# Layer 1 of a four-layer decoder on one Trainium2 core: half 0 of the cross attention centred and projected amid half 1's recurrence

## What is computed

```
# L1_attn, a gated linear recurrence
gate, u = split(x @ Wi)
u = causal_conv4(u) + conv_b
forget, inp = split(u @ Wg + bg)
alpha = exp(-8 * softplus(forget_base) * sigmoid(forget))
beta = sqrt(1 - alpha**2 + 1e-6)
h[t] = alpha[t] * h[t-1] + beta[t] * sigmoid(inp[t]) * u[t]
x = x + (gelu(gate) * h) @ Wo

# L1_xattn, on the normalized x, 16 heads (a reshape without a transpose)
Q, K, V = xn @ Wq + bq, ctx @ Wk + bk, ctx @ Wv + bv
x = x + softmax(causal(Q K^T * sqrt(8))) V
```

## Time and profile before

| | us |
|---|---|
| median of 3 runs (lowest to highest) | 1304.92 (1300.38 to 1306.22) |
| the profiled execution: time | 1302.31 |
| the profiled execution: span of the trace | 1300.4 |
| layer 1, half 1's gates to the first scores | about 444 to 480 in the trace |
| layer 1, attention steps | about 479 to 567 in the trace |

### The profile page before, as it was taken

How to read it: one execution, slowest core, us unless ns; L and a number is a source line. 1 busy time by engine, 2 the same in 40 slices (tenths; PEclk the granted TensorE clock), 3 DMA queues, 4 the chain that set the end, 5 groups by cost and what they waited for, 6 DMA issues and landing times. The chain is left out here.

```text
span 1300.4 us, 22279 instructions
## 1 busy us (share of the span) xinstructions
PE 1014.2 (78%) x8221; PEld 764.4 (59%) x8221; DVE 772.3 (59%) x1870; ACT 656.5 (50%) x1688; POOL 337.1 (26%) x440
## 2 busy tenths in 40 slices
PE   5357877783779657788998988997679961878998
PEld 4324444452776235677986765775358850546898
DVE  4789995873314656743336665674777667763422
ACT  1158885661445634745537765775113223753433
POOL 2254542762222223500002332333410031111000
PEclk9679898885889877998999999999789995987999
DMA  7200000002555000020000000000220000000000
GB/s 245 82 1 1 2 1 17 2 1 70 152 148 204 1 1 2 2 98 1 1 1 1 2 1 2 1 2 9 102 95 36 1 1 0 2 1 1 1 1 17
DMA packets 31978, 42.46 MB, mean 33 GB/s; under 512 B 7592, under 2 KB 25632, under 8 KB 30592
## 3 DMA queue, kind: packets, MB, share of 16 engines
q1 hardware_dynamic: 30848, 38.95, 9.1%
q0 software_dynamic: 1024, 2.10, 0.5%
HBM read 35.54 MB, written 5.51 MB: 32 GB/s over the span
## 5 line engine op out<-in xcount | busy, mean ns | idle before, releaser
L1287 ACT ACTIVATE arena<-bank,w_L_ffn_b1T 128x512 f32<-128x512 f32 x128 | 86.7, 687 | 101.0 <-PE bank L1229 100.6
L1264 PEld LDWEIGHTS bank<-bufB,arena 128*128 128x128 f32 x1024 | 119.1, 192 | 2.3
L1264 PE MATMUL bank<-bufB,arena 128*128 128x128 f32 x1024 | 119.8, 275 | 0.0
L2511 ACT ACTIVATE arena<-arena 128x128 f32<-128x128 f32 x256 | 99.2, 390 | 20.0 <-DVE arena L2538 20.0
L293 POOL TENSOR_TENSOR norm_rstd<-norm_std,minus_half 128x4 f32<-128x4 f32 x24 | 25.4, 1059 | 321.6 <-DVE norm_std L288 321.6
L2522 POOL TENSOR_TENSOR arena<-arena 128x512 f32<-128x512 f32 x64 | 66.5, 1040 | 150.1 <-DVE arena L2571 150.1
L1324 DVE SCALAR_TENSOR_TENSOR x<-bank,gate_c,x 128x128 f32<-128x128 f32 x128 | 36.0, 344 | 116.8 <-PE bank L1264 116.5
L545 ACT ACTIVATE arena<-arena 128x128 f32<-128x128 f32 x256 | 80.4, 396 | 43.6 <-DVE arena L553 43.6
L1229 PE MATMUL bank<-x_high,w_low 128*128 128x512 f32 x200 | 86.3, 432 | 9.7 <-DVE w_low L1238 7.1
L1229 PE MATMUL bank<-x_high,w_high 128*128 128x512 f32 x200 | 81.1, 406 | 0.0
L1229 PE MATMUL bank<-x_low,w_high 128*128 128x512 f32 x200 | 81.0, 405 | 0.0
(11 more groups left out here) (489 smaller groups left out, 2591.6 us busy)
## 6 DMA issues: line engine op xcount, KB each, us to landing
bufB<-in_L_ffn_w SPq DMA_DIRECT2D x28, 256.0 KB
bufA<-in_L_ffn_w SPq DMA_DIRECT2D x2, 2048.0 KB, 9.9
bufB<-in_L_ffn_W SPq DMA_DIRECT2D x2, 2048.0 KB
bufB<-in_L_ffn_w SPq DMA_DIRECT2D x2, 2048.0 KB
bufA<-in_L_ffn_Wgu SPq DMA_DIRECT2D x1, 2304.0 KB, 9.0
bufA<-in_L_attn_Wqkv SPq DMA_DIRECT2D x1, 2048.0 KB, 8.7
rows<-blank SPq DMA_DIRECT2D x2, 960.0 KB, 6.9
results<-arena SPq DMA_DIRECT2D x6, 256.0 KB
```

The lines of the kernel that those rows point to most:

```text
L1264: i = pe.matmul(bank[:, j * P:(j + 1) * P], h[:, f, j * P:(j + 1) * P], w2[:, u * FF + f * P:u * FF + (f + 1) * P], start=f == 0, stop=f = ...
L1287: act.activation(m["h"][k % 2][:, f, :], banks[f][:, :], ACT.Gelu, bias=b1[:, c:c + 1]).then_inc(g["hidden"].sem, 1)
L2511: o = act.activation(tile, tile, ACT.Exp, bias=b2["mn"][n % 8][:, j:j + 1], scale=-1.0, accum_out=b2["sm"][n % 8][:, j:j + 1])
```

## The change

Half 0's centring goes ahead of beta's square on DVE. ACT copies `xnT` before the square root and moves out products 12 and 13 behind it. DVE moves out product 15 ahead of the scan. PE makes the four query products of half 0 between product 15 and the output projection of half 1; ACT moves out queries 0 and 2 in the recurrence stage, DVE moves out 1 and 3 between the scan and the add. Banks of queries 1 and 2 are exchanged. In step 0 of the attention, each of the four copies of `vh` comes behind one mask and maximum, in place of all four behind the last. No operation is added or left out.

```diff
@@ layer1_recurrence_pe
             turn_x_pe(pe, "L1_xattn", 0, 4)
             for i in range(12, 16):
                 layer1_keys_values_pe(pe, i)
+
+            pe.wait_ge(*norm["L1_xattn"]["xn0"](1))
+            pe.wait_ge(*r1m[1].out(7))
+            layer1_queries_pe(pe, 0, 0)
+            layer1_queries_pe(pe, 0, 1)
+            pe.wait_ge(*kv1m.out(14))
+            layer1_queries_pe(pe, 0, 2)
+            pe.wait_ge(*kv1m.out(15))
+            layer1_queries_pe(pe, 0, 3)
             recurrence_out_pe(pe, 1)
@@ recurrence_gates_act
-            for i in (8 * h + 4, 8 * h + 5):
-                layer1_keys_values_out(act, "A", i)
+            if h:
+                keep_xnT(act, "A", "L1_xattn", 0, 4)
+            else:
+                for i in (4, 5):
+                    layer1_keys_values_out(act, "A", i)
             act.wait_ge(*g["beta_squared"](h + 1))
             act.activation(t["beta"], t["beta"], ACT.Sqrt, bias=edge[:, :]).then_inc(g["beta"].sem, 1)
+            if h:
+                for i in (12, 13):
+                    layer1_keys_values_out(act, "A", i)
@@ layer1_recurrence_act
             layer1_keys_values_out(act, "A", 14)
+            for f4 in range(4):
+                layer1_queries_out(act, "A", 0, f4)
@@ layer1_recurrence_dve
             layer1_keys_values_out(dve, "V", 11)
+            centre_dve(dve, "L1_xattn", 0)
             recurrence_beta_dve(dve, 1)
-            centre_dve(dve, "L1_xattn", 0)
+            layer1_keys_values_out(dve, "V", 15)
             recurrence_scan_dve(dve, 1)
-            layer1_keys_values_out(dve, "V", 15)
+            for f4 in range(4):
+                layer1_queries_out(dve, "V", 0, f4)
             recurrence_add_dve(dve, 1)
@@
-        Q1_BANKS = (2, 0, 1, 3, 7, 6, 7, 6)
+        Q1_BANKS = (2, 1, 0, 3, 7, 6, 7, 6)
@@ layer1_cross_pe
-            pe.wait_ge(*norm["L1_xattn"]["xn0"](1))
-            pe.wait_ge(*r1m[1].out(7))
-            pe.wait_ge(*kv1m.out(15))
-            pe.wait_ge(*kv1m.out(14))
-            for f4 in range(4):
-                layer1_queries_pe(pe, 0, f4)
@@ layer1_cross_act
-            keep_xnT(act, "A", "L1_xattn", 0, 4)
-            for f4 in range(4):
-                layer1_queries_out(act, "A", 0, f4)
@@ layer1_cross_dve
-            for f4 in range(4):
-                layer1_queries_out(dve, "V", 0, f4)
             dve.wait_ge(*g["vh_edge"](1))
+            def values_kept(n):
+                dve.wait_ge(*g["vh_turned"](n + 1))
+                dve.tensor_copy(c1["vh"][n // 4][:, 16 * (n % 4):16 * (n % 4) + 16, 0:HD],
+                                banks[7][:, :].rearrange("p (a c) -> p a c", c=32)[:, :, 0:HD]).then_inc(g["vh"].sem, 1)
...
                     dve.tensor_reduce(mx, t3, AX.X, ALU.max).then_inc(g["peak"].sem, 1)
+                    if v == 0:
+                        values_kept(r)
                 for use, n in EDGE_USES[v]:
                     if use == "vh":
-                        dve.wait_ge(*g["vh_turned"](n + 1))
-                        dve.tensor_copy(...)
+                        if v:
+                            values_kept(n)
                         continue
```

More of the change, by code:

```diff
@@ L2199, in layer1_cross_dve @@
                     dve.tensor_reduce(mx, t3, AX.X, ALU.max).then_inc(g["peak"].sem, 1)
+                    if v == 0:
+                        values_kept(r)
                 for use, n in EDGE_USES[v]:
                     if use == "vh":
-                        dve.wait_ge(*g["vh_turned"](n + 1))
-                        dve.tensor_copy(c1["vh"][n // 4][:, 16 * (n % 4):16 * (n % 4) + 16, 0:HD],
-                                        banks[7][:, :].rearrange("p (a c) -> p a c", c=32)[:, :, 0:HD]).then_inc(
-                                            g["vh"].sem, 1)
+                        if v:
+                            values_kept(n)
                         continue
```

## The result

The changed kernel took 1286.24 us (median of 4 runs, 1286.16 to 1290.8) against 1302.73 us for the kernel before beside it (1300.38 to 1306.22): a ratio of 0.9886, 95% interval 0.9855 to 0.9916.

What follows compares the result with a forecast made beforehand. Between 451 and 567 a chain of waits across engines bounds the kernel, behind 567 PE. Gains of 8.1 us to the first mask and 3.6 in step 0 sum to 11.7, so 1304.92 becomes 1293.2 us, range 1288 to 1299.5.

Steps and rivals of the forecast that it cites:

- The chain from the Exp to the statistics: Waits across engines from half 1's Exp for alpha to its attention statistics; forecast to shorten by 11.7 us.
- Steps 1 and 2: Recurrence: centring early on idle DVE costs nothing; ACT's square root, with table loaded before its input, ends at 457.65.
- The row's price of a table switch: ACT ahead of the root: 1.32 us from one ACTIVATE's end to the next one's start, against the skill's 2.66.
- Step 3: New wait: DVE moves out product 15, taken as 1.5 us on PE, before the scan, which starts 461.35, not 465.07.
- Steps 4 and 5: Four queries hidden beside the scan, ending 464.4 to 466.5; then half 1's projection at the full clock, 1.95 us.
- Rival B: Projection runs at the low clock, 3.78 us, so add and POOL come 1.8 us later; 1295.0 us, chance 0.17.
- Rival C's second case: Product 15 holds the scan until 465, as before; 5.1 us gained, 1299.8 us; chance 0.12 for all of C.
- Step 6: First mask waits for POOL's border clearing behind the add, until 472.2; 8.1 us earlier than before.
- Step 7: Attention step 0: copies between masks hide transposes; four rounds take 6.4 us in place of 9.98, a gain of 3.6.
- The sum: Whole program: 8.1 + 3.6 = 11.7 us earlier, all that follows hanging on that chain; 1304.92 becomes 1293.2 us.
- How the numbers follow: Range and chances: 1288 (copies overlapping, 4 us of spread) to 1299.5; faster 0.87, the same 0.09, slower 0.04.
- Rivals D and E: Behind 567: D, something else fixes the end, 1304.9 us, chance 0.05; E, low clock later, up to 1313, chance 0.06.

Runs made afterwards that it cites:

- e7: Changed kernel with product 15 in bank 6 and queries 2 and 3 in banks 4 and 6; ratio to the kernel before 0.9882.
- e1: Changed kernel run once more without edit, beside the kernel before; ratio 0.9916.
- e9: Changed kernel run a third time without edit, beside the kernel before on another chip; ratio 0.9897.
- e15: Changed kernel repeated without edit in the last group of runs, beside the kernel before; ratio 0.9880.
- e10: Changed kernel plus eight unread PE matmuls between products 14 and 15; ratio to the kernel before 0.9949.
- e11: e8 plus eight unread PE matmuls ahead of the projection; ratio to the kernel before 0.9865.
- e14: e8 plus four unread PE matmuls ahead of the projection; ratio to the kernel before 0.9863.
- e13: Changed kernel plus four unread PE matmuls between products 14 and 15; ratio to the kernel before 0.9906.
- e12: e8 run once more without further edit; ratio to the kernel before 0.9885.
- e8: Changed kernel with e7's banks, and POOL clearing the first half of vh's borders early, behind half 0's recurrence; ratio to the kernel before 0.9854.

## Why the prediction was off, step by step

**The chain from the Exp to the statistics** was right in its waits and their order, and its length was off by 0.1 us: 11.6 for 11.7.

**Steps 1 and 2** held: root at 3.34 us from the Exp's start, measured 3.35. The row's price of a table switch stood: the root started 1.54 us behind the copy of `xnT`, 0.23 of it a wait for DVE. The Trainium skill's 2.66 us ("ScalarE: Activation LUTs", "What ACT_TABLE_LOAD costs") does not agree with this trace either.

**Step 3** named the wait and gave product 15 too little: from PE's start to DVE's move it took 458.34 - 456.34 = 2.0 us, not 1.5, since the whole product ran at the low clock. Even the bound for that case, 1.7 us, was short of the 1.93 measured. The multiply ahead of the scan came at 8.45 us from the Exp, forecast 8.19.

**Steps 4 and 5** held: the queries were hidden, and the projection took 2.05 to 2.13 us. The margin was thin. My 1.02 us for a query at the full clock came from a row whose window has 0.90 granted; at 1.00 the four take 3.70 us in e7, 0.92 each. But in e1, e9 and e15 they ran at a low clock in part (5.55 to 5.69 us for the four) and ended only 0.4 to 0.6 us before the gate's multiply did. Rival B (3.78) did not come in any of the four traces, though e7 and e10 show that its mechanism is real: part of that is luck, since e10's projection fell to it behind a stand of 2.40 us and the first trace's, behind 1.88, did not. Rival C's second case did not come either: product 15 let the multiply start at 8.45 us from the Exp, not at the 11.8 of its premise. The scores of the first trace did run at 2.09 us, hidden behind POOL.

**Step 6** held: mask at 19.41, forecast 19.04. **Step 7** gave 6.07 us for the four rounds, not 6.4: the copies overlap their neighbours, the bound of 3.9 us that I had named. The two small errors cancel, which is luck: 7.7 + 3.9 = 11.6 for 8.1 + 3.6.

What failed is the step from this chain to the whole program, in "The sum" and "How the numbers follow". It put everything outside the stretch at nothing, set the whole change on the median shown, 1304.92, as if that were exact, and allowed at the low end 4 us of spread between executions (1304.92 - 12.0 - 4 is 1288.9, rounded down to 1288). The same kernel's median with one run more was 1302.73, so 2.2 us of the miss of 7.0 is that median. The first trace places another 4.6 us ahead of and behind the changed stretch (2.4 and 2.2), where repeats of one kernel differ by as much (the changed kernel took 808.0 to 814.8 us behind, the kernel before 810.1 to 813.5); behind the stretch this goes with the granted clock. One of the four first runs took 1290.8 us, where the sum on 1302.73 puts it (1291.0); the other three lay at 1286.2. So two terms of the sum were mis-sized: the base, 2.2 us too high, and the part outside the stretch, put at nothing and measured at 4.6 in that trace. Whether some of those 4.6 us belongs to the change on average is not settled (2.6 +- 1.7 us by the pooled ratios less the stretch); no run shows a cause in the change for them. Rivals D and E fell: no trace gave the gain back behind the stretch beyond the scatter.

## What to carry to other kernels

Follow a move of work through every in-order queue that it passes, name what is late next, and price that: here both new waits, 4.25 and 3.17 us, could be read ahead from bank assignments and from one POOL wait, and taking them away was worth 5 us of the stretch more. Count distances from a station just ahead of the change, and give a range for the whole program the scatter that repeats show outside the stretch, some 7 us here behind it alone, rather than that of three runs. When a stand is taken out of one place, look where PE stands next, for the clock goes with it.

## What of the hardware was not expected

The same 16 matmuls cost up to twice as much behind a stand: the projection took 1.95 us without one (e11), 2.05 behind 0.30 (e14), 2.13 behind 1.88 (changed kernel, first trace), 2.46 behind 2.43 (e13), 3.79 behind 2.40 (e10), and 2.64, 2.74 and 3.78 all behind 3.93 (e12, e8, e7). So the length of the stand alone doesn't say it; the moment at which the clock fell does. In e8, e12 and e13 it was 1.00 through the whole stand and fell during the projection (0.72, 0.75 and 0.80 over it). In e7 and e10 it fell already in the stand (0.87 and 0.96 over it), and the whole projection ran at 0.50. Windows over stand and projection of e7:

```profile
440.04:443.97 3.93, 0.00 (x1) 0.01 (x1) 3.86 (x5) 3.91 (x13) 0.00 (x0) 0.87 0.00 0
443.97:447.70 3.73, 3.73 (x20) 3.51 (x20) 1.72 (x2) 1.23 (x1) 0.00 (x0) 0.50 0.02 4
```

e7 and e8 have the same instructions on PE up to there, so this moment is not set by them alone; what sets it, no run here shows.

Four unread matmuls, 3.7 us of PE work, paid for themselves where they fitted the stand of 3.9 us: e14's stretch is 1.6 us shorter than e8's. In the changed kernel four brought 0.4 us (e13). Eight, at 7.13 us, outlasted the stand and cost more than they gave: 3.4 us in e10, 1.3 in e11.
